# An attention product in three fp32r parts, x2 added on GpSimd, and two engine lists in a new order

## The reference

```python
h = layernorm(x) * (1 + ca) + sa
q, k, v = split(h @ w_qkv + b_qkv)                  # 8 heads of 64
attn = softmax(einsum('bhld,bhle->bhde', q, k) / 8)
out = einsum('bhld,bhde->bhle', v, attn) @ w_fc + b_fc + h
x = x + ga * (layernorm(out) * gamma + beta)        # x2
h = layernorm(x) * (1 + cb) + sb
k = h_mixed_k @ W_k.T                                # token shift mixes h with the token before
x = x + gb * sigmoid(h_mixed_r @ W_r.T) * (relu(k)**2 @ W_v.T)
```

## Time and profile before

| | us |
|---|---|
| median of 3 runs (lowest to highest) | 691.06 (689.15 to 691.09) |
| profiled execution, its own time | 690.6 |
| its span, first to last instruction | 688.9 |
| TensorE busy in the span | 670.7 (97%) |
| VectorE busy | 561.0 (81%) |
| ScalarE busy | 393.8 (57%) |
| GpSimd busy | 317.5 (46%) |

### The profile page before, as it was taken

One profiled execution on the slowest core, in us unless ns is written; L12 is line 12 of the kernel. 1 busy time (PEld: TensorE's weight loads), 2 busy tenths in 40 slices (PEclk: granted clock), 3 DMA queues, 4 the chain that ended last, 5 costly groups with the idle time before them and its releaser, 6 DMA issues.

```text
span 688.9 us, 11754 instructions
## 1 busy us (share of the span) xinstructions
PE 670.7 (97%) x3712; PEld 539.4 (78%) x3712; DVE 561.0 (81%) x1254; ACT 393.8 (57%) x871; POOL 317.5 (46%) x520
## 2 busy tenths in 40 slices
PE   7988999999999999999999999999999999999896
PEld 6777886888778887879868887788878788687674
DVE  5693999789887998889887898979988898658973
ACT  1424575566754675474855667546754747547662
POOL 5272864573254642565335742646325753214320
PEclk9989999999999999999999999999999999999999
DMA  8849345485836666572855849366665528628225
GB/s 316 232 152 222 103 131 123 77 212 97 209 74 142 163 135 147 99 167 92 198 113 79 219 91 213 67 141 158 145 136 99 107 72 173 123 37 179 37 31 91
DMA packets 90984, 93.02 MB, mean 135 GB/s; under 512 B 4224, under 2 KB 89000, under 8 KB 90960
## 3 DMA queue, kind: packets, MB, share of 16 engines
q0 software_dynamic: 33264, 33.03, 32.6%
q1 hardware_dynamic: 55344, 55.97, 25.6%
q10 hardware_dynamic: 2352, 3.73, 1.5%
HBM read 42.84 MB, written 33.10 MB: 110 GB/s over the span
## 4 chain that ended last, share of the span: by engine, by line
PE 86%; DVE 7%; POOL 2%; DMA 2%; issue 1%; ACT 1%; SPq 0%; DVEq 0%; POOLq 0%
PE work L1335 14%; PE work L1318 14%; PE att L1285 13%; PE gram L1267 11%; PE gram L1398 4%; PE att L1370 4%; PE work L1151 4%; PE tr L1260 4%; PE work L1153 4%; PE work L1152 4%; PE tr L1302 4%; PE att L1389 2%; PE gram L1380 1%; PE att L1318 1%; DVE st L907 1%
## 5 line engine op out<-in xcount | busy, mean ns | idle before, releaser
L471 POOL TENSOR_TENSOR rs<-ve,neg_half 128x4 f32<-128x4 f32 x32 | 41.6, 1300 | 161.4 <-DVE ve L917 161.4
L1285 PE MATMUL att<-m_sb,z_t 128*128 128x256 f32 x496 | 112.4, 380 | 1.6 <-issue 0.8
L1335 PE MATMUL work<-mx,w_k_t 128*128 128x512 f32 x236 | 106.2, 592 | 0.0
L1285 PEld LDWEIGHTS att<-m_sb,z_t 128*128 128x128 f32 x496 | 92.4, 190 | 16.9 <-issue 5.7
L1318 PE MATMUL work<-w_r_t,mx 128*128 128x256 f32 x464 | 105.7, 381 | 0.0
L1318 PEld LDWEIGHTS work<-w_r_t,mx 128*128 128x128 f32 x464 | 85.9, 190 | 11.1
L1267 PE MATMUL gram<-z 128*128 128x256 f32 (+1 forms) x512 | 90.7, 331 | 0.0
L1267 PEld LDWEIGHTS gram<-z 128*128 128x128 f32 x512 | 81.1, 194 | 6.9
L934 DVE SCALAR_TENSOR_TENSOR mx<-t_buf,mu_col,h2t 128x512 f32<-128x512 f32 x120 | 84.3, 765 | 1.1
L654 ACT ACTIVATE sq<-att 128x256 f32<-128x256 f32 x124 | 46.1, 383 | 64.1 <-PE att L1285 64.1
L1335 PEld LDWEIGHTS work<-mx,w_k_t 128*128 128x128 f32 x236 | 44.8, 190 | 44.1 <-issue 42.6
(11 more groups left out here) (170 smaller groups left out, 1283.6 us busy)
## 6 DMA issues: line engine op xcount, KB each, us to landing
x_in<-in_L_attn_x_dram SPq DMA_DIRECT2D x32, 512.0 KB, 4.8
x<-rows SPq DMA_DIRECT2D x32, 512.0 KB, 3.4
x<-in_L_attn_x_dram POOLq DMA_DIRECT2D x32, 512.0 KB, 8.9
out_dram<-x SPq DMA_DIRECT2D x31, 512.0 KB, 5.1
out_dram<-y POOLq DMA_DIRECT2D x29, 512.0 KB, 6.2
rows<-row_scratch SPq DMA_DIRECT2D x16, 128.0 KB, 4.1
rows<-row_scratch SPq DMA_DIRECT2D x8, 256.0 KB, 3.8
wqkv_sb<-in_L_attn_w_qkv_dram ACTq DMA_DIRECT2D x1, 1536.0 KB, 9.7
```

Of the source, the lines that this page charges most:

```text
L1285: ins = mm(att_banks(j, alone)[q][:, (t % 2) * D:(t % 2 + 1) * D], z_t[:, j, k, t * P:(t + 1) * P], m_sb[:, k], start=(k == 0), stop=(k == ...
L1335: ins = mm(k_banks(alone)[dh][:], w_k_t[:, ch, rows_dh], mixed(j, alone)[1][:, ch], start=(ch == 0), stop=(ch == KD - 1))
```

## The change

The attention product is taken by mm3. For that z_t is kept as two fp32r parts, z_hi (the copy that ScalarE made of z_t) and z_lo (a new step of VectorE, low_z), and m_sb is split into m_hi and m_lo by two more VectorE instructions ahead of m_ready. The transpose banks are given free by z_lo_ready instead of z_t_ready. make_x2 is cut in two: make_t stays on VectorE, and the addition to x2 goes to GpSimd as add_x2 (not in the last row). VectorE's list and GpSimd's list are put in another order; prep_wv goes from the row's front to behind the fourth addition. z_t's room is no longer lent to mix in the last row, and k_hi and k_lo have one buffer instead of two. The diff, cut to these parts:

```diff
-        z_t = sb("z_t", [P, CH, KD, CT])
+        z_hi, z_lo = (part(n, [P, CH, KD, CT]) for n in ("z_hi", "z_lo"))
-        k_hi, k_lo = (part(n, [P, 2, KD, CT]) for n in ("k_hi", "k_lo"))
+        k_hi, k_lo = (part(n, [P, KD, CT]) for n in ("k_hi", "k_lo"))
...
+            def add_x2(b, j):
+
+                pool.wait_ge(t_done, CH * b + j + 1)
+                pool.wait_ge(x2_filled[j], 16 * (b + 1))
+                nc.gpsimd.tensor_tensor(x2[:, j], t_buf[:], x2[:, j], ALU.add).then_inc(x2_ready, 1)
...
                 rstd_o(b, 0)
                 if not first:
                     add_y(b - 1, 2)
+                add_x2(b, 0)
+                if first:
+                    rstd_a(n, 2)
+                else:
                     fill_x2(b, 2)
                 rstd_2(b, 0)
+                rstd_o(b, 1)
+                add_x2(b, 1)
                 if first:
-
-                    rstd_o(b, 1)
-                    rstd_a(n, 2)
-                    rstd_2(b, 1)
-                    rstd_o(b, 2)
                     rstd_a(n, 3)
-                else:
-                    prep_wv(n)
-                    rstd_o(b, 1)
-                    rstd_2(b, 1)
-                    rstd_o(b, 2)
+                rstd_o(b, 2)
+                rstd_2(b, 1)
+                if not first:
                     add_y(b - 1, 3)
+                add_x2(b, 2)
+                if not first:
                     fill_x2(b, 3)
                 rstd_2(b, 2)
                 rstd_o(b, 3)
-                if first:
-                    prep_wv(n)
+                add_x2(b, 3)
                 add_y(b, 0)
                 fill_x2(n, 0)
+                prep_wv(n)
                 rstd_2(b, 3)
...
-            def make_x2(b, j, mixes=None, alone=False):
+            def make_t(b, j, mixes=None, alone=False):
...
+                wait_past(dve, x2_ready, i)
...
+            def low_z(b, j):
+
+                i = CH * b + j
+                for h in range(KD):
+                    dve.wait_ge(z_hi_ready, 2 * i + h + 1)
+                    nc.vector.tensor_tensor(z_lo[:, j, h], tr[h][:], z_hi[:, j, h].bitcast(F32),
+                                            ALU.subtract).then_inc(z_lo_ready, 1)
...
-                                        res[:].rearrange("p k d -> p (k d)"), ALU.add).then_inc(m_ready, 1)
+                                        res[:].rearrange("p k d -> p (k d)"), ALU.add).then_inc(m_step, 1)
+                dve.wait_ge(m_step, 2 * b + 1)
+                nc.vector.tensor_copy(m_hi[:], m_sb[:]).then_inc(m_step, 1)
+                dve.wait_ge(m_step, 2 * b + 2)
+                nc.vector.tensor_tensor(m_lo[:], m_sb[:], m_hi[:].bitcast(F32), ALU.subtract).then_inc(m_ready, 1)
...
                 take_g(b)
                 prep_now(n)
-                make_x2(b, 0)
-                stats_2(b, 0)
+                low_z(n, 0)
+                make_t(b, 0)
                 if first:
                     stats_a(n, 2)
                     stats_a(n, 3)
-                    make_x2(b, 1)
-                    stats_2(b, 1)
+                else:
+                    prep_qk(n)
+                stats_2(b, 0)
+                if not first:
+                    make_z(n, 2)
+                    low_k(b - 1, 3)
+                low_z(n, 1)
+                make_t(b, 1)
+                if first:
                     make_z(n, 2)
                 else:
-                    prep_qk(n)
-                    low_k(b - 1, 3)
-                    make_z(n, 2)
-                    make_x2(b, 1)
-                    stats_2(b, 1)
+                    gate_o(b - 1, 3)
                 mix(b, 0)
+                stats_2(b, 1)
+                low_z(n, 2)
                 if first:
                     prep_qk(n)
-                else:
-                    gate_o(b - 1, 3)
                 take_wvf(b)
-                make_x2(b, 2)
+                make_t(b, 2)
+                make_z(n, 3)
                 stats_2(b, 2)
                 low_k(b, 0)
-                make_z(n, 3)
                 mix(b, 1)
+                low_z(n, 3)
                 gate_o(b, 0)
-                make_x2(b, 3)
+                make_t(b, 3)
                 mix(b, 2)
                 low_k(b, 1)
                 stats_2(b, 3)
...
             dve.wait_ge(wqkv_loaded, 16)
             prep_qk(0)
+            low_z(0, 2)
             rows_b()
+            low_z(0, 3)
             centre_fc()
...
                 for h in range(KD):
+                    if j > 0 and (first or j == 1):
+                        pe.wait_ge(z_lo_ready, 2 * i - 1 + h)
...
-                            ins = mm(att_banks(j, alone)[q][:, (t % 2) * D:(t % 2 + 1) * D], z_t[:, j, k, t * P:(t + 1) * P], m_sb[:, k],
-                                     start=(k == 0), stop=(k == KD - 1))
+                            ins = mm3(att_banks(j, alone)[q][:, (t % 2) * D:(t % 2 + 1) * D],
+                                      (z_hi[:, j, k, tile], z_lo[:, j, k, tile], m_hi[:, k], m_lo[:, k]),
+                                      start=(k == 0), stop=(k == KD - 1))
...
                 for h in range(KD):
+                    if not last and j < CH - 1:
+                        pe.wait_ge(z_lo_ready, 2 * (i + 1 + CH) + 1 + h)
```

More of the change, by code:

```diff
@@ L128, in adaln_block @@
         m_sb = sb("m_sb", [P, KD, D])
+        m_hi, m_lo = (part(n, [P, KD, D]) for n in ("m_hi", "m_lo"))
         x_in = sb("x_in", [P, CH, NT, D])
         z = sb("z", [P, 2, NT, D])
[L133 removed]
+        z_hi, z_lo = (part(n, [P, CH, KD, CT]) for n in ("z_hi", "z_lo"))
         st_a = sb("st_a", [P, CH, NT, 6])
@@ L162, in y_buf, with k_split, mixed @@
             return x_in[:, j] if alone else y[:, j % 2]
-        def k_split(j):
-            return k_hi[:, j % 2], k_lo[:, j % 2]
+        def k_split(j, alone):
+            return (z_hi[:, 0], z_hi[:, 1]) if alone and j == CH - 1 else (k_hi, k_lo)
         def o_banks(j, alone):
             return att if alone and j == CH - 1 else work[0:2]
-        def mixed(j, alone):
-            return (z_t[:, 2 * j - CH], z_t[:, 2 * j - CH + 1]) if alone and j >= CH // 2 else (xr[:, j % 2], xk[:, j % 2])
+        def mixed(j):
+            return xr[:, j % 2], xk[:, j % 2]
         wmod_sb = h2t[:, :, 1:1 + 6 * D]
@@ L708, in row_steps @@
                 squares(b, 0)
-                copy_z_t(n, 0)
+                copy_z_hi(n, 0)
                 prep_base_qk(n)
@@ L712, in row_steps @@
                     squares(b, 1)
-                    copy_z_t(n, 1)
+                    copy_z_hi(n, 1)
                     make_z2(b, 0)
@@ L729, in row_steps @@
                 make_z2(b, 2)
-                copy_z_t(n, 3)
+                copy_z_hi(n, 3)
                 copy_gram(n)
@@ L772, in _ @@
             load_more()
-            copy_z_t(0, 0)
-            copy_z_t(0, 1)
+            copy_z_hi(0, 0)
+            copy_z_hi(0, 1)
             act.wait_ge(last_loaded, 16)
@@ L898, in make_x2 @@
                 ins.then_inc(t_done, 1)
+            def make_x2(b, j, mixes):
+                i = CH * b + j
+                make_t(b, j, mixes=mixes, alone=(j > 0))
                 dve.wait_ge(t_done, i + 1)
@@ L917, in stats_2, with mix @@
                 nc.vector.tensor_scalar(ve_2[:, s], ag_2[:, s, :, 1], EPS_LN, None, ALU.add).then_inc(ve_2_done, 1)
-            def mix(b, j, made=None, alone=False):
+            def mix(b, j, made=None):
                 i = CH * b + j
-                if not alone:
-                    wait_past(dve, r_done, 2 * i - 2)
-                    wait_past(dve, k_done, 2 * i - 2)
+                wait_past(dve, r_done, 2 * i - 2)
+                wait_past(dve, k_done, 2 * i - 2)
                 wait_past(dve, xk_mixed, i)
@@ L931, in mix @@
                 dve.wait_ge(dif_done, i + 1)
-                for n, (dst, ready) in enumerate(zip(mixed(j, alone), (xr_mixed, xk_mixed))):
+                for n, (dst, ready) in enumerate(zip(mixed(j), (xr_mixed, xk_mixed))):
                     for h in range(KD):
@@ L1097, in last_row @@
                 stats_2(b, 3)
-                mix(b, 2, alone=True)
+                mix(b, 2)
                 gate_o(b, 0)
                 low_k(b, 1, alone=True)
-                mix(b, 3, alone=True)
+                mix(b, 3)
                 gate_o(b, 1, alone=True)
@@ L1116, in _ @@
             make_z(0, 1, first=True)
+            low_z(0, 0)
             stats_a(0, 3)
@@ L1120, in _ @@
             prep_now(0)
+            low_z(0, 1)
             make_z(0, 3, first=True)
@@ L1249, in turn_and_gram @@
                 pe.wait_ge(z_ready, i + 1)
-                if first or j == 1:
-                    wait_past(pe, z_t_ready, 2 * i)
-                elif j == 0:
+                if j == 0:
                     wait_past(pe, h2_ready, 2 * CH * (b - 1))
-                else:
+                elif not first and j > 1:
                     pe.wait_ge(h2_ready, 2 * (CH * (b - 1) + j - 1))
                 for h in range(KD):
```

(8 more changed lines are left out.)

40 lines of the change are left out of this document (22 added, 18 removed).

## The result

The changed kernel takes 794.41 us (median of 4 runs, 793.49 to 796.39) beside 690.65 us for the kernel before (4 runs, same chip): ratio 1.1507, 95% interval 1.1485 to 1.1529. That is slower by 104 us; forecast were 43, with a range of up to 67. The direction held, the size did not. The profiled execution took 795.0 us with a span of 793.4.

What follows compares the result with a forecast made beforehand. TensorE was taken to bound the kernel, with no slack for VectorE's k_lo. Steady rows +34, row 0 +9.5, set-up +0.6 and last row -1.5 gave +42.6 on 690.6: 733 us, range 704 to 758.

Steps and rivals of the forecast that it cites:

- four attention blocks: TensorE's attention product per row: three fp32r products save 0.72 us per chunk, 2.9 us per row.
- first stall: TensorE's output product waits for low_k of the previous row's chunk 3: 5.1 us, 2.7 without exclusion.
- second stall: TensorE's output product of chunk 0 waits for low_k(0) on VectorE: 3.1 us, 1.8 without exclusion.
- third stall: low_k(1) on VectorE comes late behind mix(2): some 0.4 us per steady row.
- the add's 2.34 us: GpSimd's x2 add, priced from the weight preparation's first instruction in the set-up; ends 1.9 to 2.7 us.
- The clock falls too: Rival: TensorE's clock halves for 3.4 us stretches, each costing 1.7; one per steady row 743 us, two 753; chance 0.25.
- prep_wv now falls into mix(2): GpSimd's v-weight preparation meets VectorE's mix(2), which waits for the fourth add; low_k(1) some 0.4 us late.
- Row 0: First row: m's split, low_z and the adds delay VectorE until low_k(0), which TensorE waits for: +9.5 us.
- Set-up: Before the rows: low_z(0,2) and low_z(0,3) push the softmax and wv_ready; some 0.6 us reaches TensorE.
- last row: x2 add stays on VectorE; of 2.9 us saved, waits for k_lo and z2 leave about 1.5.
- TensorE stays the bound: Rival: low_k steps come in time, so TensorE's saving stays; 670 us with both in time; chance 0.07.
- No exclusion: Rival: GpSimd's add runs beside VectorE's SBUF work without holding it; 706 us; chance 0.14.

Runs made afterwards that it cites:

- experiment 10: Three-product attention with x2 adds on VectorE, VectorE's steady list reordered and v weights prepared at mix(1)'s end: 688.38 us, 0.9966 of the kernel before.
- Experiment 1: Changed kernel with prep_wv in steady rows moved on GpSimd from behind chunk 3's add to ahead of chunk 1's add: 754.02 us.
- experiment 3: Changed kernel with added, overwritten TensorE products ahead of only the first late k_lo wait of a row (chunk 3's output product): 783.45 us.
- experiment 6: Kernel before with the three-product attention alone: adds on VectorE, old order, four low_z steps put in: 708.15 us.
- experiment 9: experiment 6 with one VectorE step moved, low_k of the previous row's last chunk ahead of prep_qk: 716.85 us.
- experiment 2: Changed kernel with 6, 9 and 9 overwritten float32 products added on TensorE ahead of the three late k_lo waits: 760.39 us.

## Why the prediction was right in direction and wrong in size

By its own steps, per steady row (forecast +5.7, measured 95.55 - 80.20 = +15.35):

| step | forecast | measured |
|---|---|---|
| four attention blocks | -2.9 | -2.3 |
| first stall | 5.1 | 4.45 |
| second stall | 3.1 | 2.92 |
| third stall | 0.4 | 4.43 |
| clock | 0 | 5.8 |
| sum | 5.7 | 15.3 |

- **Right:** the bound before, the place of the stalls and VectorE's k_lo as what ends them, the add's 2.34 us (2.36 at 395.78; mean of 28 with disturbed ones 2.60), its exclusion of VectorE's SBUF-only work, and the first two stalls within 0.7 us.
- **The clock (5.8 of the missing 9.6 us).** The step that failed first is "The clock falls too": it was a rival at 0.25, with one or two stretches of 3.4 us per row, and the sum 5.1 + 3.1 + 0.4 - 2.9 has no term for it. The prediction had a row for a 2.0 us gap that left the clock alone, and took the forecast's own gaps of 5.1 and 3.1 as if they would do so too. In the changed kernel the clock fell behind all twelve gaps of 4.3 to 4.5 us in the steady rows and behind five of the six of 2.9: three falls per row, one of them 6.8 us long, and two falls of 3.4 us in the first row. The 2.0 us row was no safe ground either: in experiment 10 the clock fell behind the same gap of the last row (2.04 us; 0.50 from 645.7 to 649.0). By the Trainium skill, page "TensorE: Matmul & The Clock Gate", section "HAM oscillation — how this bites in real kernels", long waits between bursts of products bring the clock down each time; the trace agrees for the gaps of 4.3 to 4.5 us, and behind shorter ones it fell in some rows and not in others (2.94 us at 196.44 without a fall, 2.92 at 386.19 with one).
- **The third stall (4.0).** The step "prep_wv now falls into mix(2)" failed in its size: it named the right collision and put it at 0.4 without a working. By the prediction's own rows two such instructions last 2.34 to 2.62 and 1.89 us, 4.2 to 4.5 together; the gap measured 4.43, with dif at 5.83 and the rest of mix at 4.25. Experiment 1 showed that this is all of it.
- **The saving (0.6).** The price of 0.114 us per product was right for the output product. In the attention block a product takes 0.12, 24 of them 2.87 us (373.17 to 376.04 in experiment 10, 431.18 to 434.05 in the changed kernel); the saving is 0.58 per chunk.
- **The ends.** Row 0 took 94.1 us instead of 77.7, +16.4 where 9.5 were forecast: it has the third gap as well (4.43 us), and the clock stands at 0.50 from 99.1 to 105.8 and from 122.9 to 129.7. Set-up (+0.9 for 0.6) and last row (-2.2 for -1.5) came out near the forecast.
- **Rivals.** "TensorE stays the bound" did not happen, and experiment 10, where it does, gave 688 and not 670. "No exclusion" is refuted by the stretched rows above.

## What to carry to other kernels

Price an engine's list by where the due step stands in it, not by its busy sum: VectorE's own work was to rise by 1.0 us a row, and three late steps cost 11.8. (Its busy time rose by 8.6, because a stretched instruction counts as busy.) When a forecast contains a new gap on TensorE longer than any that the trace shows at full clock, put a fall of the clock into the sum itself. Before an addition goes from VectorE to GpSimd, look at what VectorE would do meanwhile; if that is SBUF-only work or the consumer of the sum, nothing was won here in any of three orders.

## What was not expected of the hardware

- The length of one gap does not decide the clock. In the steady rows of the changed kernel it fell behind all gaps of 4.3 to 4.5 us. Behind gaps of 2.9 to 3.0 us it fell in some rows and not in others (changed kernel, experiments 1 and 3). Behind 2.3 to 2.4 us it stayed at 1.00 in five steady rows of experiment 6 and fell in one. In experiment 9 it fell in all six, where two gaps of up to 2.0 and 1.0 us stand close together. A stretch at 0.50 lasted 3.4 or 6.8 us in these rows.
- Products whose results nobody reads, put into the gaps, kept the clock at 1.00 and shortened the row by 5.5 us (experiment 2).
- A three-product block into the attention banks takes 0.12 us per product, the same shape in the output product 0.114 to 0.12.
